# Attention steps of a two-layer kernel: the first diagonal score block moves to a place between the two transposes of the step two places before it

## The chip, the cores and the metric

The kernel runs on one core of one Trainium2 chip. The metric is the device time of one execution in microseconds (us), as the median of several runs. The engines are called PE (TensorE: matmuls and transposes), DVE (VectorE), ACT (ScalarE), POOL (GpSimd) and SP (which issues DMAs).

## What is computed

Four sequences of 512 tokens, 128 features wide, pass through four stages: relative-position attention, a mixture of 8 experts, a gated recurrence, and a mixture of 14 experts. Each adds its input and normalizes. The change touches the attention alone:

```python
q = xh @ Wq + bq;  k = xh @ Wk + bk;  v = xh @ Wv + bv          # 8 heads of 16
content = einsum('bqhd,bkhd->bhqk', q + u_bias, k)
pos_score = rel_shift(einsum('bqhd,khd->bhqk', q + v_bias, p))
attn = softmax((content + pos_score) / sqrt(e), axis=-1)
ctx = einsum('bhqk,bkhd->bqhd', attn, v) @ Wo + bo
```

The relative shift makes scores left of the diagonal, on it and right of it come from different operands, so the 512 scores of a row of queries are made in pieces.

## The kernel before

The attention is cut into 64 **steps** (STEPS). Step s takes one sequence, one group of four heads, a tile of 128 queries (number i, 0 to 3) and two of the group's heads (0 and 1 here). A head's operands lie in 32 partitions, so its score matmuls use 32 rows of the PE array, and the two heads of a step use different rows.

All engines walk one common list of events, written by `plan_attention`, and each picks out what is its own. PE's events are:

- `score s`: for each head a diagonal block of 128 columns (L892, into bank DA: head 0 in its first 128 columns, head 1 in the next), the part before the diagonal (L898, 128 x i columns) and the part from the diagonal on (L903, 512 - 128 x i columns). It is written in this order: diagonal of head 0, L898 of head 1 and of head 0, L903 of head 1 and of head 0, diagonal of head 1. The last one waits until the first has finished (s_d0), since both write the bank DA.
- `turn s, jj`: four transposes (L921) of head jj's 128x512 probabilities into bank PT. ACT copies PT to SBUF (L708). PT is a single bank, so the transposes of the next head wait for that copy (s_pTs).
- `values`: attn times v, for probabilities transposed four or more steps earlier (L936), on 32-column tiles of the array.
- `job`: projections and transposes for the next sequences and groups, on the full array (L973 to L1020).

DVE, for each score event: it copies the lower triangles of both diagonal blocks from DA over the scores (L1309, counted by s_diag), adds a correction (L1317), and takes the negated row maxima (L1321). ACT: exp of each head (L701, after DVE's maxima), the copies of PT (L708), and a few jobs. Every engine works its list in order.

In the loop of the plan, iteration s is: turn (s, 0); values; turn (s, 1); exp of step s + 1; the jobs due; score s + 2. The score event waits for exp of step s (its banks), and for s_diag, DVE's copy of step s + 1, since DA is single. For the first steps of a sequence and group it waits for the queries (s_q, s_q0) and keys (s_kb).

A fp32 matmul stands in the trace as two MATMUL rows (two passes), a transpose as one. In the first four iterations there are no values, and a matmul of no use (`warm`, L855) follows each turn.

Of the kernel before, what the change touches and what calls it, by code (L numbers as in the profile page):

```python
# [14 lines left out]
P = 128  # L15
# [5 lines left out]
NG = H // HG  # L21
# [7 lines left out]
HP = 32  # L29
STEPS = B * NG * 2 * TB  # L30
# [46 lines left out]
def plan_attention():  # L77

    jobs, plan = [], []

    def put(event):
        if event[0] == "job":
            jobs.append(event[1:])
            plan.append(("job", len(jobs) - 1))
        else:
            plan.append(event)

    per = NG * 2 * TB  # L90
    later = {}

    def at(step, *events):
        later.setdefault(step, []).extend(events)

    for e in (("stats", 0), ("cols", 0), ("kd", 0), ("job", "pem", 0), ("job", "wqT", 0), ("normz", 0), ("job", "bias", 0),
              ("job", "zT", 0), ("job", "fold", 0), ("job", "k", 0, 0), ("kb", 0, 0), ("job", "t1a", 0, 0),
              ("job", "t2a", 0, 0), ("qa", 0), ("job", "corr", 0), ("delta", 0, 0), ("job", "t1r", 0, 0),
              ("job", "t2r", 0, 0), ("kd", 1)):
        put(e)  # L100
    for i in range(1, TB):
        put(("delta", 0, i))
    at(0, ("job", "v", 0))
    at(1, ("job", "k", 0, 1), ("kb", 0, 1))
    at(2, ("job", "t1", 0, 1))
    at(3, ("job", "t2", 0, 1), ("q", 0, 1), ("xbo", 0))
    at(16, ("job", "wo", 0))
    at(6, ("numbers", 0))
    for b in range(1, B):
        base = per * (b - 1)  # L110
        first = 3 if b == 1 else 0
        at(base if b == 1 else base - 1, ("stats", b))
        at(base + first, ("normz", b))
        at(base + first + 1, ("job", "zT", b))
        at(base + first + 2, ("job", "k", b, 0), ("kb", b, 0))
        at(base + first + 3, ("job", "k", b, 1), ("kb", b, 1))
        at(base + 7, ("job", "t1", b, 0))
        at(base + 8, ("job", "t2", b, 0), ("q", b, 0))
        at(base + 9, ("job", "corr", b))
        at(base + 10, ("job", "t1", b, 1))  # L120
        at(base + 11, ("job", "t2", b, 1), ("q", b, 1))
        at(base + 13, ("job", "v", b), ("xbo", b))
    for m in range(1, B * NG):
        for i in range(TB):
            at(8 * m + 2 * i - 6, ("delta", m, i))
    for b in range(B):
        base = per * b
        at(base + 12, ("job", "ctxT", 2 * b))
        at(base + 20, ("job", "ctxT", 2 * b + 1))
        at(base + 21, ("job", "cxT", b))  # L130
        at(base + 22, ("job", "out", b), ("post", b))
        at(base + 23, ("post2", b))
        at(base + 24, ("rms", b))
        at(base + 28, ("xn2", b))
        at(base + 30, ("job", "xT", b))
        at(base + 31, ("job", "logits", b))
        at(base + 32, ("job", "rank", b))
        at(base + 33, ("scatter", b))
    plan += [("score", 0), ("exp", 0, 0), ("exp", 0, 1), ("qr", 0), ("ids", 0), ("score", 1)]
    for s in range(STEPS + 2 * per + 2):  # L140
        if s < STEPS:
            plan.append(("turn", s, 0))
        if TB <= s < STEPS + TB:
            plan.append(("values", s // TB - 1, s % TB))
            if (s // TB - 1) % 2 == 1 and s % TB == TB - 1:
                plan.append(("ctx", (s // TB - 1) // 2))
        if s < STEPS:
            plan.append(("turn", s, 1))
        if s + 1 < STEPS:
            plan += [("exp", s + 1, 0), ("exp", s + 1, 1)]  # L150
        for e in later.pop(s, []):
            put(e)
        if s + 2 < STEPS:
            plan.append(("score", s + 2))
    assert not later, later
    return jobs, plan
# [19 lines left out]
def build(nc, x_in, ca_in, ct_in, cb_in, wp0_in, wp1_in, out):  # L176
    jobs, plan = plan_attention()
# [22 lines left out]
    with ExitStack() as ctx:  # L200
# [29 lines left out]
        def by_batch(width):  # L230
            nonlocal at
            v = arena1[:, at:at + 2 * NG * width].rearrange("p (r g q) -> p r g q", r=2, g=NG)
            at += 2 * NG * width
            return v

        ka, kb, qb, qa = by_batch(S), by_batch(S), by_batch(S), by_batch(QW)
# [123 lines left out]
        s_score = sem("s_score")  # L360
        s_d0 = sem("s_d0")
        s_diag = sem("s_diag")
# [9 lines left out]
        s_q0 = sem("s_q0")  # L372
        s_q = sem("s_q")
        s_qs = sem("s_qs")
        s_kb = sem("s_kb")
# [60 lines left out]
        DA, PT, CTX, JOB = bank[4], bank[5], bank[6], bank[7]  # L436
        NHALF = STEPS // TB

        def place_of_step(s):

            m, u = divmod(s, 2 * TB)
            return m // NG, m % NG, s // TB, u // 2, 2 * (u % 2)
# [402 lines left out]
        def _(eng):  # L845
# [11 lines left out]
            def ranks(l, b, into):  # L857
# [9 lines left out]
                    mm = eng.matmul(into[:, TB * E:(TB + 1) * E], C("ones"), upto_tile[:, 0:E, TB], start=True, stop=True)  # L867
                return mm

            used = {}  # L870
            for kind, *w in plan:
                if kind == "score":
                    s = w[0]
                    b, g, _, i, j0 = place_of_step(s)
                    r = b % 2
                    if s >= 2:
                        eng.wait_ge(s_exp, 2 * (s - 2) + 2)
                    else:
                        for name in (("t1a", "t2a"), ("k", "t1r"))[s]:
                            eng.wait_ge(*after(name, 0, 0))  # L880
                    if s:
                        eng.wait_ge(s_diag, s)
                    if i == 0 and j0 == 0:
                        eng.wait_ge(*(s_q, NG * (b - 1) + g + 1) if b else (s_q0, 1 + 2 * g))
                        eng.wait_ge(s_kb, NG * b + g + 1)
                    if s == 2:
                        eng.wait_ge(s_q0, 2)
                    mine, split = slice(i * P, (i + 1) * P), i * P

                    def diagonal(jj):  # L890
                        rows = slice(HP * (j0 + jj), HP * (j0 + jj + 1))
                        return eng.matmul(DA[:, jj * P:(jj + 1) * P], qa[rows, r, g, mine], ka[rows, r, g, mine],  # L892
                                          start=True, stop=True)

                    def before(jj):
                        rows = slice(HP * (j0 + jj), HP * (j0 + jj + 1))
# [6 lines left out]
                        eng.matmul(bank[2 * (s % 2) + jj][:, split:S], qb[rows, r, g, mine], kb[rows, r, g, split:S],  # L903
                                   start=True, stop=True)

                    diagonal(0).then_inc(s_d0, 1)
                    before(1)
                    before(0)
                    behind(1)
                    behind(0)  # L910
                    eng.wait_ge(s_d0, s + 1)
                    diagonal(1).then_inc(s_score, 1)
                    if s == 0:
                        warm(1, PT[:, 0:2 * P])
                elif kind == "turn":
                    s, jj = w
# [8 lines left out]
                elif kind == "values":  # L925
                    v, t = w
                    m, hh = divmod(v, 2)
                    b, g = divmod(m, NG)
# [5 lines left out]
                    for j in range(HG):  # L934
# [3 lines left out]
                                        start=(t == 0), stop=(t == TB - 1))  # L938
                    mm.then_inc(s_pv, 1)
                elif kind == "job":  # L940
# [37 lines left out]
                    elif name == "v":  # L978
                        eng.wait_ge(*after("zT", a[0]))
                        for t in range(TB):  # L980
                            mm = eng.matmul(bk[:, t * D:(t + 1) * D], xnT[:, t * P:(t + 1) * P],
                                            A("wv").rearrange("p (h d) -> p h d", h=H)[:, :, 0:DH],
                                            start=True, stop=True)
                    elif name[0] == "t":
                        b, g = a
# [20 lines left out]
                    elif name == "out":  # L1006
                        eng.wait_ge(*after("cxT", a[0]))
                        eng.wait_ge(*after("wo", 0))
                        for t in range(TB):
                            mm = eng.matmul(bk[:, t * D:(t + 1) * D], cxT[:, t * P:(t + 1) * P], wo[:, :],  # L1010
                                            start=True, stop=True)
# [4 lines left out]
                    elif name == "logits":  # L1016
                        eng.wait_ge(*after("xT", a[0]))
                        eng.wait_ge(s_cb, 16)
                        for t in range(TB):
                            mm = eng.matmul(bk[:, t * E0:(t + 1) * E0], xnT2[:, t * P:(t + 1) * P], C("gate"),  # L1020
                                            start=True, stop=True)
# [49 lines left out]
            for kind, b, *half_of in middle:  # L1071
                r = b % 2
# [20 lines left out]
                elif kind == "gate":  # L1093
                    c = half_of[0]
                    eng.wait_ge(s_u, NC * (b + 1))
                    for q, name in enumerate(("wb", "wa", "wc")):
# [3 lines left out]
                        for k in range(NC):  # L1100
                            mm = eng.matmul(bank[4 + v % 2], R(name, k * INNER + c * P, P), uu[:, r, k, :],  # L1101
                                            start=(k == 0), stop=(k == NC - 1))
# [19 lines left out]
                elif kind == "logits":  # L1122
                    eng.wait_ge(s_copied, copied[("router", b)])
                    for t in range(TB):
                        mm = eng.matmul(bank[6][:, t * E1:(t + 1) * E1], xnT2[:, t * P:(t + 1) * P], rw[:, :],
                                        start=True, stop=True)
# [596 lines left out]
```

## Time and profile before

| | us |
|---|---|
| median of 3 runs | 553.13 (547.18 to 553.98) |
| the profiled execution, its device time | 551.84 |
| the profiled execution, its span | 550.0 |
| outside the span | 1.84 |
| from the first transposes of step 0 to those of step 62 | 19.4 to 263.5 |

The span is the time from the first instruction to the last. Rows of a timeline give start and length; the length of a PE row is modelled and includes the way through the array, so rows of pipelined matmuls overlap, and PE at 82% busy is not at its peak.

### The profile page before, as it was taken

How to read it: one execution, taken by the hardware profiler on the slowest of the kernel's cores; microseconds unless marked ns; L12 is line 12 of the kernel's file. 1: busy time of each engine (PE TensorE's matmuls, PEld its weight loads, DVE VectorE, ACT ScalarE, POOL GpSimd, SP SyncE). 2: the span in 40 equal slices, each digit the busy share in tenths (PEclk: the TensorE clock that was granted, in tenths of full speed). 3: DMA queues.
4: the chain of work that ended last, by engine and by line, in shares of the span. 5: the costliest groups of instructions: out<-in, count | busy, mean ns of one | idle time of the engine just before them, and what ended most of it. 6: DMA issues, size and time to landing. Idle time of an engine off the chain costs nothing. (4 is left out here: it accounts for less than half of the span.)

```text
span 550.0 us, 9872 instructions
## 1 busy us (share of the span) xinstructions
PE 452.6 (82%) x3109; PEld 317.3 (58%) x3109; DVE 356.1 (65%) x893; ACT 267.4 (49%) x547; POOL 249.2 (45%) x260
## 2 busy tenths in 40 slices
PE   8798999999999999999857799738979798428870
PEld 7565666656656566666434799613454466327760
DVE  4976676676876777667434466367486566638882
ACT  2356567666666565777401355517546222025653
POOL 3452563446572862440033154442445466425771
PEclk9999999999999999999886899958989978659995
DMA  8499999999999000000040230090000000013405
GB/s 308 109 174 172 170 195 345 189 190 186 194 181 159 3 1 7 16 2 1 2 143 19 63 89 28 13 378 34 0 2 1 1 21 15 24 46 77 103 19 154
DMA packets 69395, 52.72 MB, mean 96 GB/s; under 512 B 3238, under 2 KB 67245, under 8 KB 68704
## 3 DMA queue, kind: packets, MB, share of 16 engines
q1 hardware_dynamic: 66656, 47.84, 44.0%
q0 software_dynamic: 2688, 4.25, 2.6%
q8 instruction: 26, 0.43, 0.4%
q14 instruction: 25, 0.20, 0.1%
HBM read 21.30 MB, written 32.09 MB: 97 GB/s over the span
## 5 line engine op out<-in xcount | busy, mean ns | idle before, releaser
L708 ACT ACTIVATE arena<-banks 128x512 f32<-128x512 f32 x128 | 76.4, 597 | 86.3 <-PE banks L921 86.1
L921 PE MATMUL banks<-ca,work 128*128 128x128 f32 x512 | 82.2, 283 | 18.2 <-ACT arena L708 14.3
L701 ACT ACTIVATE work<-banks,nmax 128x512 f32<-128x512 f32 x128 | 80.7, 686 | 13.7 <-DVE nmax L1321 13.5
L921 PEld LDWEIGHTS banks<-ca,work 128*128 128x128 f32 x512 | 53.6, 140 | 55.5 <-issue 43.0
L1321 DVE TENSOR_REDUCE nmax<-banks 128x2 f32<-128x1024 f32 x64 | 78.3, 1224 | 2.2
L903 PE MATMUL banks<-arena 32*128 32x512 f32 (+3 forms) x256 | 60.1, 435 | 0.0
L892 PEld LDWEIGHTS banks<-arena 32*128 32x128 f32 x256 | 41.2, 184 | 30.4 <-issue 23.2
L892 PE MATMUL banks<-arena 32*128 32x128 f32 x256 | 55.2, 295 | 0.6 <-DVE corr L1401 0.6
L1309 DVE COPY_PREDICATED banks<-ca,banks 128x256 f32<-128x256 uint32 x64 | 27.2, 426 | 38.1 <-PE banks L892 37.9
L1046 PE MATMUL banks<-t,arena 128*128 128x128 f32 x300 | 47.1, 295 | 3.9 <-ACT t L815 1.0
L1101 PE MATMUL banks<-arena 128*128 128x512 f32 x96 | 45.4, 623 | 1.2 <-POOL arena L680 1.2
L1046 PEld LDWEIGHTS banks<-t,arena 128*128 128x128 f32 x300 | 40.0, 202 | 9.3 <-issue 7.6
L1055 PE MATMUL banks<-arena,work 128*128 128x128 f32 x300 | 43.3, 280 | 0.9 <-ACT work L822 0.6
L898 PE MATMUL banks<-arena 32*128 32x128 f32 (+2 forms) x192 | 43.8, 401 | 0.0
L749 ACT ACTIVATE work<-banks,arena 128x128 f32<-128x128 f32 x92 | 26.3, 368 | 31.8 <-PE banks L1046 31.8
L936 PE MATMUL banks<-arena 128*32 128x256 f32 x512 | 41.8, 402 | 0.0
L642 POOL DMA_INDIRECT returned<-arena x29 | 29.3, 1011 | 23.0 <-DVE arena L1462 13.1
L1055 PEld LDWEIGHTS banks<-arena,work 128*128 128x128 f32 x300 | 38.5, 196 | 1.7 <-ACT work L822 1.1
L547 POOL DMA_INDIRECT regions<-xc,pos x16 | 16.4, 1026 | 48.5 <-DVE pos L1202 44.7
L600 POOL TENSOR_TENSOR arena<-ca,corr 128x512 f32<-128x512 f32 x32 | 33.5, 1052 | 10.2 <-DVE nmax L1321 7.3
L633 POOL DMA_INDIRECT returned<-work,arena x23 | 22.6, 983 | 32.2 <-DVE work L1451 17.5
L903 PEld LDWEIGHTS banks<-arena 32*128 32x128 f32 x256 | 35.8, 185 | 1.0
(221 smaller groups left out, 828.9 us busy)
## 6 DMA issues: line engine op xcount, KB each, us to landing
regions<-zeros SPq DMA_DIRECT2D x15, 1040.0 KB, 18.4
regions<-zeros SPq DMA_DIRECT2D x9, 1032.0 KB, 19.9
arena<-wp_in SPq DMA_DIRECT2D x1, 4624.0 KB, 26.3
arena<-wp_in SPq DMA_DIRECT2D x1, 4494.0 KB, 15.9
arena<-ct_in SPq DMA_DIRECT2D x2, 1024.0 KB, 9.7
arena<-regions SPq DMA_DIRECT2D x29, 65.0 KB, 1.9
arena<-cb_in SPq DMA_DIRECT2D x1, 1660.0 KB, 8.2
arena<-regions SPq DMA_DIRECT2D x23, 64.5 KB, 1.9
```

What stands on the lines that cost most here:

```text
L600: eng.tensor_tensor(delta[:, i, :, :], A("ident").unsqueeze(1).broadcast_to([P, HG, P]), corr[:, b % 2, i, g * HG:(g + 1) * HG].unsqueeze( ...
L701: eng.activation(prob[:, r, :], bank[r], ACT.Exp, bias=nmax[:, s % 2, jj:jj + 1]).then_inc(s_exp, 1)
L708: eng.activation(probT[:, v % 2, j0 + jj, :, i % 2 * P:(i % 2 + 1) * P], PT.rearrange("p (t q) -> p t q", t=TB), ACT.Copy).then_inc(s_pTs, 1)
L892: return eng.matmul(DA[:, jj * P:(jj + 1) * P], qa[rows, r, g, mine], ka[rows, r, g, mine], start=True, stop=True)
L898: eng.matmul(bank[2 * (s % 2) + jj][:, 0:split], qa[rows, r, g, mine], ka[rows, r, g, 0:split], start=True, stop=True)
L903: eng.matmul(bank[2 * (s % 2) + jj][:, split:S], qb[rows, r, g, mine], kb[rows, r, g, split:S], start=True, stop=True)
L921: mm = eng.transpose(PT[:, t * P:(t + 1) * P], prob[:, 2 * (s % 2) + jj, t * P:(t + 1) * P], ident)
L936: mm = eng.matmul(CTX[HP * j:HP * (j + 1), 2 * P * hh:2 * P * (hh + 1)], vv[:, b % 2, t, h * HP:(h + 1) * HP], probT[:, v % 2, j, t, :], s ...
L1046: mm = eng.matmul(bank[r][:, c * P:(c + 1) * P], wbuf[:, r, c * P:(c + 1) * P], xTs[:, r, :], start=True, stop=True)
L1055: mm = eng.matmul(bank[3 + r][:, 0:D], hT[:, r, c * P:(c + 1) * P], wbuf[:, r, F + c * D:F + (c + 1) * D], start=(c == 0), stop=(c == CH - 1))
L1101: mm = eng.matmul(bank[4 + v % 2], R(name, k * INNER + c * P, P), uu[:, r, k, :], start=(k == 0), stop=(k == NC - 1))
L1321: eng.tensor_reduce(nmax[:, s % 2, :], pair, AX.X, ALU.max, negate=True).then_inc(count(s_fixed), 1)
```

## The change

The diagonal block of head 0 becomes an event of its own, `diag s`. It is taken out of `score s` and stands in iteration s - 2 behind turn (s - 2, 0) and the values, ahead of turn (s - 2, 1). It takes the waits for s_diag and for queries and keys with it. The rest of `score s` keeps its place, its order and the wait for exp. For steps 0 and 1 `diag` stands right ahead of `score`. No other engine's list changes.

```diff
-    plan += [("score", 0), ("exp", 0, 0), ("exp", 0, 1), ("qr", 0), ("ids", 0), ("score", 1)]
+    plan += [("diag", 0), ("score", 0), ("exp", 0, 0), ("exp", 0, 1), ("qr", 0), ("ids", 0), ("diag", 1), ("score", 1)]
     for s in range(STEPS + 2 * per + 2):
         if s < STEPS:
             plan.append(("turn", s, 0))
...
             plan.append(("values", s // TB - 1, s % TB))
...
+        if s + 2 < STEPS:
+            plan.append(("diag", s + 2))
         if s < STEPS:
             plan.append(("turn", s, 1))
...
+                if kind == "diag":
+                    s = w[0]
+                    b, g, _, i, j0 = place_of_step(s)
+                    if s:
+                        eng.wait_ge(s_diag, s)
+                    if i == 0 and j0 == 0:
+                        eng.wait_ge(*(s_q, NG * (b - 1) + g + 1) if b else (s_q0, 1 + 2 * g))
+                        eng.wait_ge(s_kb, NG * b + g + 1)
+                    if s == 2:
+                        eng.wait_ge(s_q0, 2)
+                    diagonal(s, 0).then_inc(s_d0, 1)
+                elif kind == "score":
...
-                    diagonal(0).then_inc(s_d0, 1)
                     before(1)
                     before(0)
                     behind(1)
                     behind(0)
                     eng.wait_ge(s_d0, s + 1)
-                    diagonal(1).then_inc(s_score, 1)
+                    diagonal(s, 1).then_inc(s_score, 1)
```

PE's list in the steady part, before: the transposes (L921) of a step's head 0, the values (L936), the transposes of head 1, a job (L990), the score blocks of the step two places on.

```order
L921 MATMUL banks<-ca,work 128x128 [waits s_pTs,s_exp]
L921 MATMUL banks<-ca,work 128x128 x3
L936 MATMUL banks<-arena 32x256 x4
L921 MATMUL banks<-ca,work 128x128 [waits s_pTs,s_exp]
L921 MATMUL banks<-ca,work 128x128 x3
L990 MATMUL banks<-xnT,wt 128x512 [waits s_outa,s_outd]
L892 MATMUL banks<-arena 128x128 [waits s_diag,s_exp]
L898 MATMUL banks<-arena 128x256 x2
L903 MATMUL banks<-arena 128x256 x2
L892 MATMUL banks<-arena 128x128 [waits s_d0]
```

The same place in the changed kernel, where the transposes are L927, the values L942, the job L996, the parts before and from the diagonal L905 and L910, and both diagonal blocks L875.

```order
L927 MATMUL banks<-ca,work 128x128 [waits s_pTs,s_exp]
L927 MATMUL banks<-ca,work 128x128 x3
L942 MATMUL banks<-arena 32x256 x4
L875 MATMUL banks<-arena 128x128 [waits s_diag]
L927 MATMUL banks<-ca,work 128x128 [waits s_pTs,s_exp]
L927 MATMUL banks<-ca,work 128x128 x3
L996 MATMUL banks<-xnT,wt 128x512 [waits s_outa,s_outd]
L905 MATMUL banks<-arena 128x256 [waits s_exp]
L905 MATMUL banks<-arena 128x256
L910 MATMUL banks<-arena 128x256 x2
L875 MATMUL banks<-arena 128x128 [waits s_d0]
```

The diagonal block of head 0, with its wait for s_diag, now stands ahead of the second set of transposes, and that set with everything behind it is queued behind the wait.

PE's list in iteration 0, before: both sets of transposes with their warm matmuls, the job for v (L981), the score blocks of step 2.

```order
L921 MATMUL banks<-ca,work 128x128 [waits s_exp]
L921 MATMUL banks<-ca,work 128x128 x3
L855 MATMUL banks<-ca 128x256
L921 MATMUL banks<-ca,work 128x128 [waits s_pTs,s_exp]
L921 MATMUL banks<-ca,work 128x128 x3
L855 MATMUL banks<-ca 128x256
L981 MATMUL banks<-ca,xnT 128x128 [waits s_outa,s_outd]
L981 MATMUL banks<-ca,xnT 128x128 x3
L892 MATMUL banks<-arena 128x128 [waits s_q0,s_diag,s_exp]
```

The same in the changed kernel, where the warm matmul is L857 and the job L987.

```order
L927 MATMUL banks<-ca,work 128x128 [waits s_exp]
L927 MATMUL banks<-ca,work 128x128 x3
L857 MATMUL banks<-ca 128x256
L875 MATMUL banks<-arena 128x128 [waits s_q0,s_diag]
L927 MATMUL banks<-ca,work 128x128 [waits s_pTs,s_exp]
L927 MATMUL banks<-ca,work 128x128 x3
L857 MATMUL banks<-ca 128x256
L987 MATMUL banks<-ca,xnT 128x128 [waits s_outa,s_outd]
L987 MATMUL banks<-ca,xnT 128x128 x3
L905 MATMUL banks<-arena 128x128 [waits s_exp]
```

The wait for DVE's copy of step 1 (s_diag) has moved from behind the job to ahead of the second transposes.

## Rows read from the trace of the kernel before

**Rows 1.** The page's first part: each engine's busy time and instructions.

```profile
PE 452.6 (82%) x3109; PEld 317.3 (58%) x3109; DVE 356.1 (65%) x893; ACT 267.4 (49%) x547; POOL 249.2 (45%) x260
```

**Rows 2.** Windows, the attention: length, busy by engine, then PE clock, DMA.

```profile
38.00:262.00 224.00, 210.17 (x1758) 139.92 (x1755) 160.69 (x307) 142.90 (x243) 105.42 (x106) 1.00 0.76 126
```

**Rows 3.** Waits, whole span: us in total, times, longest.

```profile
PE banks L921 <- ACT arena L708: 14.3, 64, 0.6
```

**Rows 4.** Timeline of PE, iteration 36: start, length, what [idle before].

```profile
166.33 0.66 PE L921 MATMUL banks<-ca,work 128*128 128x128 f32 x4
166.92 0.64 PE L936 MATMUL banks<-arena 128*32 128x256 f32 x8
167.77 0.63 PE L921 MATMUL banks<-ca,work 128*128 128x128 f32 x4 [0.21 <-ACT arena L708]
168.23 0.60 PE L1001 MATMUL banks<-ca,arena 128*128 128x128 f32 x4
168.76 0.37 PE L892 MATMUL banks<-arena 32*128 32x128 f32 x1
168.77 0.58 PE L898 MATMUL banks<-arena 32*128 32x384 f32 x1
168.97 0.27 PE L892 MATMUL banks<-arena 32*128 32x128 f32 x1
...
169.52 0.48 PE L903 MATMUL banks<-arena 32*128 32x128 f32 x3
...
169.85 0.27 PE L892 MATMUL banks<-arena 32*128 32x128 f32 x1
170.05 0.66 PE L921 MATMUL banks<-ca,work 128*128 128x128 f32 x4
```

**Rows 5.** Timeline of ACT, the same iteration.

```profile
167.02 0.60 ACT L708 ACTIVATE arena<-banks 128x512 f32<-128x512 f32 x1 [0.97 <-PE banks L921]
168.43 0.60 ACT L708 ACTIVATE arena<-banks 128x512 f32<-128x512 f32 x1 [0.81 <-PE banks L921]
168.93 1.26 ACT L701 ACTIVATE work<-banks,nmax 128x512 f32<-128x512 f32 x2
```

**Rows 6.** Timelines: DVE's copy in iterations 36 and 39, PE's values in 39.

```profile
166.45 0.43 DVE L1309 COPY_PREDICATED banks<-ca,banks 128x256 f32<-128x256 uint32 x1 [0.48 <-PE banks L892]
...
178.52 0.64 PE L936 MATMUL banks<-arena 128*32 128x256 f32 x8
...
178.74 0.41 DVE L1309 COPY_PREDICATED banks<-ca,banks 128x256 f32<-128x256 uint32 x1
```

**Rows 7.** Timelines of ACT and PE, an iteration without a job.

```profile
227.13 1.26 ACT L701 ACTIVATE work<-banks,nmax 128x512 f32<-128x512 f32 x2
...
227.86 0.66 PE L921 MATMUL banks<-ca,work 128*128 128x128 f32 x4
```

**Rows 8.** Timeline of PE, iterations 0 and 1.

```profile
20.86 0.63 PE L921 MATMUL banks<-ca,work 128*128 128x128 f32 x4 [0.34 <-ACT arena L708]
...
22.74 0.37 PE L892 MATMUL banks<-arena 32*128 32x128 f32 x1
...
24.83 0.65 PE L921 MATMUL banks<-ca,work 128*128 128x128 f32 x4 [0.73 <-ACT work L701]
...
26.26 0.63 PE L921 MATMUL banks<-ca,work 128*128 128x128 f32 x4 [0.34 <-ACT arena L708]
```

**Rows 9.** Timeline of DVE, its copies of steps 1, 2 and 5.

```profile
21.91 0.42 DVE L1309 COPY_PREDICATED banks<-ca,banks 128x256 f32<-128x256 uint32 x1
...
26.28 0.41 DVE L1309 COPY_PREDICATED banks<-ca,banks 128x256 f32<-128x256 uint32 x1
...
40.12 0.42 DVE L1309 COPY_PREDICATED banks<-ca,banks 128x256 f32<-128x256 uint32 x1
```

**Rows 10.** Timeline of PE, transposes in iterations 4 and 5.

```profile
39.97 0.63 PE L921 MATMUL banks<-ca,work 128*128 128x128 f32 x4 [0.21 <-ACT arena L708]
...
43.05 0.66 PE L921 MATMUL banks<-ca,work 128*128 128x128 f32 x4 [0.72 <-ACT work L701]
```

More of the change, by code:

```diff
@@ L868, in ranks, with diagonal @@
                 return mm
+            def diagonal(s, jj):
+                b, g, _, i, j0 = place_of_step(s)
+                rows, mine = slice(HP * (j0 + jj), HP * (j0 + jj + 1)), slice(i * P, (i + 1) * P)
+                return eng.matmul(DA[:, jj * P:(jj + 1) * P], qa[rows, b % 2, g, mine], ka[rows, b % 2, g, mine],
+                                  start=True, stop=True)
             used = {}
             for kind, *w in plan:
-                if kind == "score":
+                if kind == "diag":
+                    s = w[0]
+                    b, g, _, i, j0 = place_of_step(s)
+                    if s:
[7 more added lines that the diff above has]
+                elif kind == "score":
                     s = w[0]
@@ L880, in _ @@
                             eng.wait_ge(*after(name, 0, 0))
[L881 to L887, printed above, removed]
                     mine, split = slice(i * P, (i + 1) * P), i * P
[L890 to L893, printed above, removed]
                     def before(jj):
```

## The prediction

> **What bounds the kernel now.** I read the busy times first: PE is the busiest engine [rows 1], and in the attention, nearly half of the span, it has work in 210 of 224 us at a granted clock of 1.00 [rows 2], the upper level of 2.4 GHz. So the question is what PE's own sequence costs there. The list of waits gives one place in each step where PE stands still for another engine: the second transposes wait for ACT's copy of PT, 64 times, 14.3 us in all [rows 3]. The timeline of one iteration shows all of it. [rows 4] is iteration 36: transposes of head 0 at 166.33, values at 166.92, 0.21 us of idling, transposes of head 1 at 167.77, a job at 168.23, the score blocks from 168.76 to 169.85, and the next iteration's transposes at 170.05 with no wait ahead of them. ACT is not late: its copies end at 167.62 and 169.03, and the first of its two exps (1.26 us for both) ends some 0.4 us before PE needs it [rows 5]. PE's order sets the pace; only the hole ahead of the second transposes is free. The change puts a matmul into this hole.
>
> **What changing the array's shape costs, read from the same rows.** Full-array work, 32-column tiles (values) and 32-row tiles (scores) never overlap. The next kind starts 0.07 us before the modelled end of the last: transposes end at 166.99 and values start at 166.92; the job ends at 168.83 and scores start at 168.76; the diagonal ends at 170.12 and transposes start at 170.05 [rows 4]. From the last 128-column pass to the next kind is 0.20 us, where passes of 128 columns in one kind follow at 0.11.
>
> The Trainium skill has this as a rule: "TensorEngine Tiling (Array Packing)", Key Properties, says that changing the tiling mode drains the engine. The trace agrees, and puts some 0.09 us on each such drain.
>
> **The moved block, where it lands.** Values of iteration 36 end at 167.56, so by that rule of the rows the diagonal can start at 167.49. Its passes stand 0.21 us apart when it opens a kind (168.76 and 168.97 [rows 4]: its weights are not yet loaded), and 0.20 us later the transposes can start: 167.90. Before they started at 167.77. They also lose a little that the idling hid: a set that starts right behind other work takes 0.66 us and one that waited for ACT 0.63 [rows 4]. So the last transposes of head 1 come 0.13 + 0.03 = **0.16 us** later. The hole was 0.28 us wide (167.49 to 167.77) and is asked to take 0.41 and a second drain.
>
> The one unseen piece is the drain from 32-column to 32-row tiles. Bounds from the nearest rows: none at all (-0.09 us), or two drains in one (+0.09). All transitions that are shown cost the same, so I take 0.09 for this one too. Per iteration this leaves 0.07 to 0.25, about 0.16.
>
> **The block, where it is taken away: nothing comes back.** The two heads of a score event run side by side. The head-0 diagonal starts at 168.76 and L898 of head 1 at 168.77, before the diagonal's second pass at 168.97 [rows 4]. Each head has 128 + 512 = 640 columns, two passes each. At 0.107 us for 128 columns that is 1.07 us, with 0.11 for the first weights 1.18; the last pass starts at 169.85 and takes 0.11, so from 168.77 to 169.96 is 1.19. Both heads fill the whole event. After the change head 0 has 512 columns left and head 1 still 640, its diagonal among them, so the event lasts as long as before. The semaphore s_d0 was long up before head 1's diagonal, so no wait goes away either.
>
> **What stands behind the late transposes.** ACT's copy of PT, then exp of the next step on ACT, and on PE the job and the score event. With a job, PE's own sequence carries the 0.16 into the next iteration. Without one (11 iterations), the next transposes start 0.05 us after exp has ended (227.13 plus half of 1.26, about 227.8, against 227.86 [rows 7]), and exp follows the copy of PT on ACT: this path carries the 0.16 as well. Iterations 4 to 61 have both values and a moved block, 58. Iterations 4 and 5 belong to the start, which leaves 56 x 0.16 = **9.0 us**.
>
> **The moved wait.** The block waits for DVE's copy of the step before it. In iteration 36 this ends at 166.88, 0.6 us early [rows 6]. In 39 DVE has first done statistics, and the copy ends at 179.15, while the block could start at 179.16 - 0.07 = 179.09 [rows 6]; with some 0.05 us for the semaphore that is 0.12 late. The same pattern is found in 23 and 55. In 55 PE idles for exp right behind, and that hole swallows it and the iteration's 0.16. So 2 x 0.12 - 0.16 = **+0.1 us**. The queries and keys of a new group are ready many us before.
>
> At the start it costs more. DVE copies step 1 only at 21.91 to 22.33 [rows 9]; the block goes at 22.44, the second transposes of iteration 0 at 22.85 in place of 20.86, the score event at 24.76 in place of 22.74, the next transposes at 26.06 in place of 24.83 [rows 8]. Now the job for v reaches DVE 0.8 us later, so its copy of step 2, 26.28 to 26.69 [rows 9], ends at 27.49; the block follows at 27.54, and the second transposes of iteration 1 at 27.95, not 26.26 [rows 8]: 1.7 us late. In iterations 2 and 3 the block fits beside the wait for ACT. In 4 the copy ends at 40.54 [rows 9], and transposes planned for 39.97 would go at 41.0, but the next ones idle 0.72 us at 43.05 [rows 10], which takes back most; 5 has another hole. Left over: 1.7 + 0.1 = **1.8 us**, with bounds of 0.5 and 2.6, as these waits partly cover each other.
>
> **Sum.** 9.0 + 0.1 + 1.8 = 10.9 us on the profiled execution: 551.84 becomes 562.7. That execution lies 1.3 us under the median, so the forecast is 553.13 + 10.9 = **564.0 us**, 1.020 times the time before. Behind the attention nothing is due at a fixed time, so the delay is carried to the end. The bounds of the drain give 5.9 to 15.9 in place of 10.9.
>
> **Rivals.**
>
> *The hole takes the block and the score event shrinks (faster).* If the two heads' matmuls really ran one behind the other, the event would lose the first diagonal's 0.21 us and PE would get it back in the 45 iterations that PE paces. From 0.16 on, what the event gives back outweighs the late transposes. With the drain at its lower bound as well, these 45 would gain 0.21 - 0.07 = 0.14 each, 6 us, and with the start absorbed the time would be about 547; with no delay at all of the second transposes it is 45 x 0.21 = 9 us, 544. Against it: L898 of head 1 starts 0.01 us after the diagonal [rows 4]. Chance 0.07, of which 0.02 is beyond 2% (under 542.1).
>
> *A draw.* Half of that, with the event back by a part: it shrinks by about the 0.11 us of first weights, and the drain is short. The steady part costs 56 x 0.05 = 3, the start 1 to 2: 557 to 558. Chance 0.08.
>
> *Matmuls start in the order written.* Then the new order (both L898, both L903, one diagonal) overlaps badly: head 0's L903 could not start before head 1's second pass of it, and by the widths of [rows 4] the event would last 0.21 us longer (1.39 in place of 1.18, for every i). With 0.16 before it this is 0.37 in 56 iterations, 21 us, and the time about 576. Against it: L898 of head 1 at 168.77 starts ahead of the earlier written second pass at 168.97 [rows 4]. Chance 0.05.
> The Trainium skill states this rule in "TensorE: Matmul & The Clock Gate", Part 3, The mechanism: matmuls start and end strictly in program order. Here the trace disagrees, by 0.2 us in the row just named.
>
> *The waits on DVE bite more often*, since every engine's timing shifts: each stall costs 0.1 to 0.5 us; 10 of them give 566 to 569. Chance 0.10.
>
> *The change does not do what it says.* PE's list shows the block in the new place; excluded.
>
> **How the numbers follow.** The forecast has 0.70. A measurement of this kernel tells about 2%, and the forecast lies on this line: 564.2 is 2% above 553.13. Its own spread, some 3 us each way from the start-up term, the drain and the runs, falls half on each side. Within 2%: half of the forecast, the draw, the gain but for its 0.02, and 0.02 of the DVE rival: 0.50. Slower by over 2%: the other half, the order rival, the rest of the DVE rival: 0.48. Faster: 0.02. The range of 557 to 569.5 leaves out the gain, the order rival and the ends of the drain's bounds, less than 2 in 10.
>
> **What would show it.** In the changed profile the second transposes start 0.34 us after the modelled end of the values (before: 0.21), with the block between them; the score event lasts as long as before; iteration 36 lasts 3.88 us where 3.72 stands now (166.33 to 170.05 [rows 4]); the transposes of step 62 start near 274.4, not 263.5. I would be wrong if the score event got shorter by 0.1 us or more, if the transposes did not move, or if iterations 0 and 1 kept their times.

## The result

| | before | changed |
|---|---|---|
| median | 551.11 us (547.18 to 553.98, 6 runs) | 560.94 us (559.62 to 564.8, 6 runs) |
| ratio | | 1.0187, 95% interval 1.0135 to 1.0238 |
| profiled execution, span | 550.0 us | 558.4 us |
| its device time | 551.84 us | 560.2 us |

The changed kernel is slower by 9.8 us in the medians; the interval of the ratio lies on both sides of 1.02. Forecast were 10.9 us more, and 564.0 us. Of the 3.1 us between 564.0 and 560.94, 2.0 are the base: the median of three runs was 553.13, that of six is 551.11.

In two later comparisons, on other chips, the same kernel had ratios of 1.0219 (1.0145 to 1.0293) and 1.0256 (1.0202 to 1.031). The ratios leave out executions more than 1.5% above the fastest of their kernel, and in the first of the two that is four of six. The medians of all executions there are 578.69 against 560.54 us (570.09 to 595.17), and 564.74 against 549.5 us: 18.2 and 15.2 us more.

The page of the changed kernel, its first part, against [rows 1]:

```profile
PE 472.9 (85%) x3109; PEld 325.9 (58%) x3109; DVE 355.9 (64%) x893; ACT 267.0 (48%) x547; POOL 249.1 (45%) x260
```

Its windows, for the stretch from iteration 4 on that answers to [rows 2], with the same columns:

```profile
42.00:274.00 232.00, 230.81 (x1752) 147.33 (x1750) 160.38 (x306) 142.68 (x243) 105.35 (x106) 1.00 0.72 119
```

DVE, ACT and POOL are busy for as long as before. PE counts as busy in 231 of 232 us, where it was in 210 of 224 [rows 2]: its holes are gone, and the stretch is still 8 us longer. A busy share says nothing of speed when what fills a hole is dearer than what it takes away elsewhere.

The timeline of PE, iteration 36 of the changed kernel (start, length, what), answers to [rows 4]:

```profile
174.63 0.66 PE L927 MATMUL banks<-ca,work 128*128 128x128 f32 x4
175.22 0.64 PE L942 MATMUL banks<-arena 128*32 128x256 f32 x8
175.79 0.48 PE L875 MATMUL banks<-arena 32*128 32x128 f32 x2
176.20 0.66 PE L927 MATMUL banks<-ca,work 128*128 128x128 f32 x4
176.69 0.60 PE L1007 MATMUL banks<-ca,arena 128*128 128x128 f32 x4
177.22 0.91 PE L905 MATMUL banks<-arena 32*128 32x384 f32 x4
177.97 0.39 PE L910 MATMUL banks<-arena 32*128 32x128 f32 x4
178.19 0.38 PE L875 MATMUL banks<-arena 32*128 32x128 f32 x2
178.51 0.33 PE L927 MATMUL banks<-ca,work 128*128 128x128 f32 x1
```

Values end at 175.86. The block (L875) starts 0.07 us before that, and the second transposes start at 176.20, 0.34 behind the values, where it was 0.21 [rows 4]. The score event runs from 177.22 to the next transposes at 178.51, 1.29 us; with the block in it, it ran from 168.76 to 170.05, also 1.29. The iteration lasts 3.88 us (174.63 to 178.51) in place of 3.72.

The timeline of ACT in the same iteration, against [rows 5]:

```profile
175.33 0.60 ACT L710 ACTIVATE arena<-banks 128x512 f32<-128x512 f32 x1 [0.97 <-PE banks L927]
176.90 0.60 ACT L710 ACTIVATE arena<-banks 128x512 f32<-128x512 f32 x1 [0.97 <-PE banks L927]
177.39 1.26 ACT L703 ACTIVATE work<-banks,nmax 128x512 f32<-128x512 f32 x2
```

The copy of PT ends at 175.93, 0.27 us before PE is ready for the bank. PE no longer waits for ACT, and ACT idles 0.97 us for PE where it was 0.81. The list of waits, whole span as [rows 3]:

```profile
PE banks L927 <- ACT arena L710: 0.4, 2, 0.2
PEld banks L875 <- DVE banks L1315: 7.8, 10, 2.2
PE banks L875 <- DVE banks L1315: 2.8, 3, 1.4
```

The 14.3 us of waits for ACT [rows 3] have turned into 0.4. The two other rows are new: the block's weight loads wait 7.8 us in all for DVE's copy, and PE itself (PE, not PEld) stands still for it in iterations 0, 1 and 4 alone, 2.8 us.

**Where the 8.4 us between the two spans arose.** Starts of the first transposes of an iteration, from the timelines:

| | before | changed | difference, and what it grew by |
|---|---|---|---|
| iteration 0 | 19.43 | 19.08 | -0.35 |
| iteration 6 | 47.58 | 51.17 | 3.59, start-up: +3.9 |
| iteration 62 | 263.55 | 275.95 | 12.40, steady part: +8.8 |
| end of the span | 550.0 | 558.4 | 8.4, later stages: -4.0 |

The steady part was forecast at 9.1, the start-up at 1.8, the later stages at nothing.

The start of the changed kernel, timeline of PE against [rows 8] (transposes at 19.08 and 22.89 for 19.43 and 20.86):

```profile
19.08 0.79 PE L927 MATMUL banks<-ca,work 128*128 128x128 f32 x4 [1.03 <-ACT work L703]
...
22.16 0.79 PE L875 MATMUL banks<-arena 32*128 32x128 f32 x2 [1.45 <-DVE banks L1315]
22.89 1.11 PE L927 MATMUL banks<-ca,work 128*128 128x128 f32 x4
...
27.70 0.66 PE L927 MATMUL banks<-ca,work 128*128 128x128 f32 x4
```

Its windows there (length, busy of PE, PEld, DVE, ACT, POOL, then clock and DMA):

```profile
18.00:19.00 1.00, 0.05 (x2) 0.00 (x0) 0.97 (x2) 0.66 (x2) 1.00 (x2) 1.00 0.00 0
19.00:20.00 1.00, 0.92 (x5) 0.92 (x6) 0.96 (x2) 0.70 (x3) 1.00 (x2) 0.73 0.00 0
20.00:22.00 2.00, 0.72 (x2) 0.00 (x0) 1.93 (x5) 0.50 (x1) 0.52 (x1) 0.50 0.00 0
22.00:26.00 4.00, 3.84 (x15) 3.43 (x16) 1.77 (x3) 1.75 (x3) 0.00 (x0) 0.50 0.91 203
26.00:27.00 1.00, 1.00 (x9) 0.79 (x10) 0.41 (x2) 0.00 (x0) 0.00 (x0) 0.85 1.28 179
```

The block stands before the second transposes and waits for DVE, as forecast: it starts 3.08 us after the first transposes, where 3.01 was forecast (22.44 against 19.43). Not forecast: the clock is granted at 0.50, the lower level of 1.2 GHz, for 7 us from about 19.5 on. A set of four transposes takes 1.11 us in place of 0.66, and iteration 0 lasts 8.6 us (19.08 to 27.70) in place of 5.4.

### The profile page after: what moved, and what is told of

It is laid out like the page before. It is cut to its first block and busy times, and to the rows that moved or that the text cites. A ratio compares the mean times of both kernels' runs of the same rounds, so it can differ in the third digit from the quotient of the medians.

```text
span 558.4 us, 9811 instructions
## 1 busy us (share of the span) xinstructions
PE 472.9 (85%) x3109; PEld 325.9 (58%) x3109; DVE 355.9 (64%) x893; ACT 267.0 (48%) x547; POOL 249.1 (45%) x260
## 5 line engine op out<-in xcount | busy, mean ns | idle before, releaser
L927 PE MATMUL banks<-ca,work 128*128 128x128 f32 x512 | 84.5, 288 | 2.4 <-ACT work L703 1.9
L875 PEld LDWEIGHTS banks<-arena 32*128 32x128 f32 x256 | 41.5, 185 | 42.3 <-issue 28.9
L927 PEld LDWEIGHTS banks<-ca,work 128*128 128x128 f32 x512 | 53.9, 141 | 19.5 <-ACT work L703 4.4
L875 PE MATMUL banks<-arena 32*128 32x128 f32 x256 | 55.6, 296 | 3.1 <-DVE banks L1315 2.8
L910 PE MATMUL banks<-arena 32*128 32x512 f32 (+3 forms) x256 | 47.0, 440 | 0.0
L1107 PE MATMUL banks<-arena 128*128 128x512 f32 x96 | 43.0, 597 | 1.2 <-POOL arena L682 1.2
L942 PE MATMUL banks<-arena 128*32 128x256 f32 x512 | 40.5, 391 | 0.0
L1444 DVE COPY arena<-arena 128x642 f32 (+1 forms) x52 | 31.3, 601 | 6.3 <-DVE work L1457 4.0
L905 PE MATMUL banks<-arena 32*128 32x128 f32 (+2 forms) x192 | 33.7, 427 | 0.0
```

Of the source, the lines that this page charges most:

```text
L875: return eng.matmul(DA[:, jj * P:(jj + 1) * P], qa[rows, b % 2, g, mine], ka[rows, b % 2, g, mine], start=True, stop=True)
L905: eng.matmul(bank[2 * (s % 2) + jj][:, 0:split], qa[rows, r, g, mine], ka[rows, r, g, 0:split], start=True, stop=True)
L927: mm = eng.transpose(PT[:, t * P:(t + 1) * P], prob[:, 2 * (s % 2) + jj, t * P:(t + 1) * P], ident)
L942: mm = eng.matmul(CTX[HP * j:HP * (j + 1), 2 * P * hh:2 * P * (hh + 1)], vv[:, b % 2, t, h * HP:(h + 1) * HP], probT[:, v % 2, j, t, :], s ...
```

## Experiments

Twelve kernels ran, four on each of three chips. A ratio compares a kernel with the kernel before on the same chip. Iteration times are differences of timeline starts between a kernel's profile and that of the kernel before. The profiles of e1_steady and e7_not0 hold a stretch of some 14 us at half clock in the midst of the attention; "without the stretch" counts 0.16 us for each of its two iterations. On the first two of these chips iteration 50 takes 0.3 to 0.8 us more in all eight kernels than in the profile of the kernel before, which is left out as well.

**1. Same columns, other shape: e3_full and e3b_rows.** Nothing is moved; a matmul of no use stands behind the values. It waits for an exp that has long ended, not for DVE. This is e3_full; e3b_rows has `eng.matmul` of 32 rows of the same operands in place of `warm`.

```diff
                     mm.then_inc(s_pv, 1)
+                    now = TB * (v + 1) + t
+                    if now < STEPS - 2:
+                        eng.wait_ge(s_exp, 2 * now + 2)
+                        warm(1, bank[2 * (now % 2)][:, 0:P])
```

> The kernel before, with one 128-column fp32 matmul of no use on the full array put between the values and the second transposes of iterations 4 to 61; nothing is moved. Theory (what costs is the change of the array's shape and the weights that it leaves bare): the matmul has as many columns as the moved block but the shape of the transposes behind it, so it starts 0.31 us after the last pass of the values, its passes take 0.06 + 0.22, and the transposes could start at about 0.58 us, where they start now (0.59, waiting for ACT). Cost 0 to 0.01 us per iteration: the time of before. Rival (what costs is the work of the block itself): the second transposes come 0.13 us or more later as in the changed kernel, 9 us in all.

> The same addition, with the matmul on 32 rows of the array as a score block has; head 0's diagonal stays in the score event as well. Theory: a second change of shape and 0.11 us of bare weights make the second transposes start 0.72 us after the last pass of the values, and since the score event gains nothing from losing the block, adding it costs as much as moving it: 0.16 us in 58 iterations, 9 us (0.163, against 0.156 in the changed kernel). Rival (the score event does give something back): adding costs more than moving by what comes back, 0.1 us or more per iteration, so 15 us or more. It waits for no copy of DVE, so nothing of the start-up.

Iteration 36 of e3_full, timeline of PE, then of e3b_rows:

```profile
167.56 0.64 PE L936 MATMUL banks<-arena 128*32 128x256 f32 x8
168.13 0.49 PE L855 MATMUL banks<-ca 128*128 128x128 f32 x2
168.45 0.60 PE L921 MATMUL banks<-ca,work 128*128 128x128 f32 x4
```

```profile
171.50 0.64 PE L936 MATMUL banks<-arena 128*32 128x256 f32 x8
172.06 0.48 PE L944 MATMUL banks<-ca 32*128 32x128 f32 x2
172.48 0.66 PE L921 MATMUL banks<-ca,work 128*128 128x128 f32 x4
```

On the full array the filler goes in at 168.13 and the transposes follow 0.32 us later: iterations last 0.02 us more, ratio 1.0005 (0.9974 to 1.0035). On 32 rows the same columns take 0.42 us to the next start, and iterations last 0.16 us more, ratio 1.0159 (1.0082 to 1.0236). So the work of the block fits into the hole; its shape does not. My count for e3_full was 0.01 to 0.02 short. And adding costs 0.16 per iteration, as moving does, so the score event gives nothing back.

**2. The score event without the block: e4_without.** This is the kernel before without head 0's block from step 1 on; that part of the scores is left out, and the kernel serves for the time alone.

```diff
-                    diagonal(0).then_inc(s_d0, 1)
+                    if s == 0:
+                        diagonal(0).then_inc(s_d0, 1)
...
-                    eng.wait_ge(s_d0, s + 1)
+                    if s == 0:
+                        eng.wait_ge(s_d0, 1)
```

> The kernel before without the diagonal block of head 0 from step 1 on (that part of the scores is left out and replaced by what stands in the bank). Theory: head 1's 640 columns set the length of the score event, so iterations get at most 0.01 us shorter (the block's place at the event's start): the time of before within 1 us. Rival 1 (the heads run one behind the other): 0.21 us less in 45 iterations, 9 us less. Rival 2 (matmuls start in written order): the new order makes the event 0.21 us longer, 9 to 12 us more.

Iteration 36, timeline of PE:

```profile
168.87 0.92 PE L898 MATMUL banks<-arena 32*128 32x384 f32 x4
169.62 0.39 PE L903 MATMUL banks<-arena 32*128 32x128 f32 x4
169.84 0.38 PE L892 MATMUL banks<-arena 32*128 32x128 f32 x2
170.16 0.66 PE L923 MATMUL banks<-ca,work 128*128 128x128 f32 x4
```

From 168.87 to 170.16 it is 1.29 us again. Iterations are 0.00 to 0.01 us shorter, ratio 1.0006 (0.9976 to 1.0036). Taking 2 x 128 columns of PE work out of every step is worth nothing while the other head's 640 columns run beside them. Both rivals fall: neither 0.21 less nor 0.21 more.

**3. The parts of the change: e1_steady, e2_start, e7_not0.** The block is moved in iterations from 6 on (e1_steady, shown), in 0 to 3, and in all but iteration 0.

```diff
-        if s + 2 < STEPS:
+        if s + 2 < STEPS and s >= 6:
             plan.append(("diag", s + 2))
...
         if s + 2 < STEPS:
+            if s < 6:
+                plan.append(("diag", s + 2))
             plan.append(("score", s + 2))
```

> The change in iterations 6 to 61 alone; in iterations 0 to 5 the block stays in the score event. Theory: 0.156 us in 56 iterations is 8.7, with 0.25 for two late copies of DVE and 0.15 swallowed in iteration 55: 8.8 us more than before; the transposes of step 62 start 8.8 us later counted from those of step 6. The granted clock stays 1.00 in the first 280 us, since nothing waits for DVE in iteration 0. Rival (the start is what costs in the medians): under 6 us.

> The change in iterations 0 to 3 alone; from iteration 4 on the block stays in the score event. Theory (the moved wait for DVE's copy stalls PE in iterations 0 and 1, and the block is free in 2 and 3): 1.7 us later at the transposes of step 2, carried on unchanged, so 1.7 us more than before in all, 3.5 if the clock falls as well. Rival (these stalls are taken back later): under 0.5 us.

> The changed kernel, with iteration 0's block (of step 2) back in its score event. Theory: without the wait for the copy of step 1, the job for v reaches DVE on time; iteration 0 takes what it took before, and only the block of step 3 waits: the copy of step 2 ends at 26.69, so the second transposes of iteration 1 start at 27.16 in place of 26.26, and iteration 1 takes 0.9 us more. The start costs 0.9 us in place of 1.7, and 8.8 us follow. Rival (what costs in iteration 0 is the block, not the wait): iteration 1 takes what it takes in the changed kernel, and the start as much.

e1_steady: ratio 1.0124 (1.0045 to 1.0204), 563.53 to 574.77 us; from iteration 6 to 62 it takes 8.8 us more than before, without the stretch. Iterations 0 to 5 take what they took. e7_not0 has the same 8.8. The steady part adds by itself, as predicted. The expectation that the clock stays at 1.00 is refuted: in e1_steady it is 0.50 for 14 us from 198.9 on. In its profile and in that of e7_not0 it is also 0.50 for 7 us from about 8 on, before iteration 0, which starts at 22.1 and 22.8 there in place of 19.4. No moved block stands so early, so low stretches also come where the change does nothing.

e2_start: ratio 1.0112 (1.0076 to 1.0148), 5 us in the medians where 1.7 or 3.5 was expected. In its profile iteration 0 takes 3.7 us more and iteration 1 0.2, with the clock at 0.50 again; iterations 4 to 62 are as before. 4 us are so accounted for, and nothing of them is taken back.

e7_not0, iteration 1, timelines of PE and DVE:

```profile
28.32 0.66 PE L929 MATMUL banks<-ca,work 128*128 128x128 f32 x4 [0.85 <-ACT work L705]
...
30.22 0.48 PE L877 MATMUL banks<-arena 32*128 32x128 f32 x2 [0.82 <-DVE banks L1317]
30.64 0.55 PE L929 MATMUL banks<-ca,work 128*128 128x128 f32 x3
...
29.76 0.41 DVE L1317 COPY_PREDICATED banks<-ca,banks 128x256 f32<-128x256 uint32 x1
```

Between the two sets of transposes lie 2.32 us in place of 1.43 (24.83 to 26.26 [rows 8]): 0.9 more, and the block starts 0.05 us after the copy ends at 30.17. Iteration 0 takes 0.1 more. So the stalls of the start are the waits for DVE, and where the clock holds they have the forecast size. Its times, 573.86 to 580.34 with a ratio of 1.0266 (1.0214 to 1.0319), contain the half-clock stretch:

```profile
60.00:70.00 10.00, 10.00 (x80) 6.35 (x80) 6.09 (x11) 5.07 (x9) 5.17 (x4) 0.98 1.30 175
70.00:75.00 5.00, 5.00 (x20) 2.37 (x22) 1.83 (x3) 2.35 (x4) 2.49 (x3) 0.50 1.41 158
```

PE was busy throughout; iterations 10 and 11 took 3.5 and 3.1 us more.

**4. The wait alone, and the clock: e10_wait, e6_again, e11_third.** e10_wait is the kernel before with

```diff
                     s, jj = w
+                    if (s, jj) == (0, 1):
+                        eng.wait_ge(s_diag, 2)
                     eng.wait_ge(s_exp, 2 * s + jj + 1)
```

The two others are the changed kernel again.

> The changed kernel once more, beside the others of this call. Asked of it: is the low granted clock at 14 to 20 us of the changed kernel's first profile bound to the change, or chance? It fell 7 us after the 14th, before PE stood still for DVE, so by the first theory (chance) it is 1.00 here, iteration 0 takes 1.2 us more than before and iteration 1 0.4 to 0.5 more, and the transposes of step 6 start 1.7 us later than before. Rival (the wait brings it): the clock falls again, and iterations 0 and 1 take 3.2 and 0.6 us more. From the transposes of step 6 to those of step 62 it is 8.8 us more than before in either case. Ratio 1.018 to 1.022.

> The kernel before, with only the wait for DVE's copy of step 1 put ahead of the second transposes of iteration 0; no block is moved. If the wait alone is what costs in iteration 0, these transposes start at 22.44 in place of 20.86, and the transposes of step 1 come 0.8 us later at a full clock. If the stall of PE is also what takes the granted clock down in all three profiles of kernels with iteration 0's block moved, the clock is 0.50 for some 7 us between 19 and 28 us here too, and it is 3 us or more. Rival (the low clock belongs to the block or is chance): the clock stays 1.00 and the cost is 0.8 us.

> The changed kernel a third time. By what the other profiles showed: low clock near 20 us at the start, iteration 0 3 us longer or more, 8.8 us from the transposes of step 6 to those of step 62, plus 6.6 us in executions with a half-clock stretch in the attention. Theory of chance at the start: iteration 0 takes 1.2 us more.

e10_wait, timeline of PE and windows:

```profile
19.66 0.66 PE L923 MATMUL banks<-ca,work 128*128 128x128 f32 x4 [1.01 <-ACT work L701]
...
22.58 1.08 PE L923 MATMUL banks<-ca,work 128*128 128x128 f32 x4 [1.83 <-DVE banks L1311]
```

```profile
20.00:22.00 2.00, 0.75 (x5) 0.35 (x3) 1.93 (x4) 0.78 (x2) 0.94 (x1) 1.00 0.00 0
22.00:23.00 1.00, 0.42 (x2) 0.42 (x3) 0.93 (x4) 0.00 (x0) 0.00 (x0) 0.83 0.00 0
23.00:26.00 3.00, 3.00 (x14) 2.75 (x12) 1.22 (x1) 1.85 (x3) 0.00 (x0) 0.50 0.98 251
26.00:27.00 1.00, 1.00 (x11) 0.84 (x11) 0.69 (x3) 0.00 (x0) 0.00 (x0) 0.96 1.22 216
```

PE stands 1.83 us for DVE, and just behind that wait the clock goes to 0.50, with no block moved: 0.83 in the window from 22 to 23 puts the fall at about 22.7, where the transposes started at 22.58. Iteration 0 takes 2.4 us more in the profile; the medians differ by 1.8 us, ratio 1.0025 (0.998 to 1.0071), which the noise covers. All five profiles of kernels in which iteration 0 waits for DVE ahead of its second transposes (the changed kernel three times, e2_start, e10_wait) have the clock going to 0.50 between 19 and 24 us, for 3 us or more; in the other eight experiments and the kernel before it does not fall there. The expectation of chance is refuted, with one reservation: the fall does not stand in one place to the wait. It came within the wait in e2_start and e6_again (20.9 and 22.1), behind its end in e10_wait and e11_third (22.7 and 23.5), and in the first profile of the changed kernel at 19.5, before this wait and after the 1.03 us one for ACT that all kernels have. So the wait is not the only thing that counts, and how it brings the low clock is not shown.

e6_again: iterations 0 and 1 take 4.4 and 2.9 us more; ratio 1.0219. Two of its executions took 594.24 and 595.17 us at a mean granted clock of 0.877, 16 us above the profiled one (578.66, clock 0.907). They have no profile, and what they hold is open. e11_third: 2.9 and 0.05, and a second low stretch of 10 us opens at 44.0, just behind a wait of 0.84 us of iteration 4's block for DVE, and adds 2.2 and 2.6 us to iterations 4 and 5; ratio 1.0256. The same wait of 0.84 us stands in the first profile of the changed kernel and in e7_not0, and the clock stays at 1.00 there. The steady part is 8.8 in both.

**5. The added matmul again: e8_rows_again.**

> The added 32-row matmul of e3b_rows again (nothing moved). Two kernels with the moved block showed a half clock for some 14 us in the midst of the attention with PE busy throughout, which cost 6.6 us. Theory A (it comes with 32-row work between the values and the transposes, in some executions): it is found here in some executions too, and the times spread over 10 us and more. Theory B (it needs the block moved away from the score event): times within 4 us of each other, 1.016 of before.

556.5 to 559.65, ratio 1.0134 (1.0087 to 1.0182), 8.7 us from iteration 6 to 62, no half-clock stretch. This favours theory B, but with four executions on a chip where e11_third had no stretch in the steady part either, it settles nothing. Nor do the times of e3b_rows: one of its four, 572.54 at a mean clock of 0.914, lies 6.5 us above its fastest, as much as a stretch costs, but so does 564.33 (clock 0.907) among those of the kernel before on that chip. What brings the stretch stays open.

**6. Filling the hole with work of the right shape: e5_jobs and e9_jobs_all.** In the kernel before, PE alone does its job of the iteration ahead of the second transposes (e9: in iterations 0 to 3 too). The other engines' lists are untouched.

```diff
-            for kind, *w in plan:
+            early_jobs, k = list(plan), 0
+            while k < len(early_jobs):
+                if early_jobs[k][0] == "turn" and early_jobs[k][2] == 1 and TB <= early_jobs[k][1] < STEPS - 2:
+                    n = k + 1
+                    while n < len(early_jobs) and early_jobs[n][0] not in ("score", "turn"):
+                        n += 1
+                    moved = [e for e in early_jobs[k + 1:n] if e[0] == "job"]
+                    rest = [e for e in early_jobs[k + 1:n] if e[0] != "job"]
+                    early_jobs[k:n] = moved + [early_jobs[k]] + rest
+                    k = n
+                else:
+                    k += 1
+            for kind, *w in early_jobs:
```

> The kernel before with another filling for the hole: in iterations 4 to 61 PE does the iteration's job between the values and the second transposes, the score event unchanged. A job has the shape of the transposes behind it. Theory (the change of shape is what made the diagonal dear): no shape change is added, PE's sequence gets shorter by 0.28 (hole) less 0.03, but ACT's copy and exp then bind: 1.89 us from the second transposes to the next iteration, so 0.18 us less in each of 45 iterations with a job, none in the other 11: 8 us faster than before, ratio 0.985. Rival (any work in the hole delays the second transposes and with them ACT, by as much as it takes away behind them): the time of before.

> As e5_jobs, with the jobs ahead of the second transposes in iterations 0 to 3 too, where the hole is 0.34 us wide behind the warm matmul. Theory: 0.3 us less in each of iterations 1 to 3 and in iteration 0 nothing, since step 1's exp is waited for there: 1 us less than e5_jobs, ratio 0.985 to 0.988. Rival: DVE binds in these iterations, the same as e5_jobs.

Iteration 36 of e5_jobs, timeline of PE:

```profile
162.96 0.66 PE L933 MATMUL banks<-ca,work 128*128 128x128 f32 x4
163.55 0.64 PE L948 MATMUL banks<-arena 128*32 128x256 f32 x8
164.12 0.66 PE L1013 MATMUL banks<-ca,arena 128*128 128x128 f32 x4
164.62 0.60 PE L933 MATMUL banks<-ca,work 128*128 128x128 f32 x4
165.15 0.37 PE L904 MATMUL banks<-arena 32*128 32x128 f32 x1
```

The job (L1013) takes the hole and the transposes follow it without one; the iteration lasts 3.52 us in place of 3.72 (the next starts at 166.48). Most iterations with a job gain 0.10 to 0.21 us, those without mostly nothing. e5_jobs: ratio 0.9886 (0.9848 to 0.9924), 5.7 us where 8 was forecast. In its profile 43 iterations gain 7.5 us in all (0.40 in two of them, many with a long job only 0.15), 17, 32 and 34 lose 0.4, and iteration 50 of this chip takes 0.7 more. e9_jobs_all: 540.69 us against 549.5, ratio **0.9828** (0.9789 to 0.9867), with 0.2, 0.5 and 0.5 us gained in iterations 1 to 3, more than expected. It is faster than the kernel before by 1.7%, and is the change to make here.

## Why the prediction was right, step by step

- **The price of a shape change, and the landing of the block.** Forecast: block 0.07 us before the modelled end of the values, transposes 0.34 after it, 0.16 us per iteration. Measured: 0.07, 0.34, and 0.158 as the mean of the 52 iterations from 6 to 61 without 23, 32, 39 and 55. The unseen switch from 32-column to 32-row tiles costs what the seen ones do; both bounds of it fall. e3_full shows that it is the shape and not the columns.
- **Nothing comes back.** The event stays at 1.29 us with the block moved or left out (e4_without), and adding equals moving (e3b_rows). The faster rival and the draw fall. So does the one by which matmuls start in the order written: the new order did not lengthen the event.
- **What stands behind.** Iterations without a job grew by 0.16 too: ACT's copy and exp carried it.
- **The late copies.** Iterations 23 and 39 grew by 0.28, that is 0.12 beyond the 0.16, and 55 by 0.01 in place of 0.16, as forecast. 32, where DVE is late too but PE idled behind it, grew by 0.04, which I had not worked out. Sum of the steady part: 9.1 forecast, 8.8 measured.
- **The start-up, mis-sized.** Forecast 1.8 us with bounds of 0.5 and 2.6; measured 3.9, 7.5 and 7.8 in the three profiles of the changed kernel, all beyond the bounds. The waits were the right ones: iteration 0's block starts 3.08 us after the first transposes for 3.01, and with a full clock iteration 1 of e7_not0 takes the 0.9 us expected of it. What failed in this term is that it prices PE's work behind the waits at the full clock: the granted clock fell to 0.50. No run shows iteration 0 with the wait and a full clock. My rival on DVE's waits priced them at 0.1 to 0.5 us each and also without the clock.
- **The later stages.** "Carried to the end" was right for the mechanism, and wrong by 4.0 us for the two profiled executions. Windows of before, then of the changed kernel, from the transposes of step 62 on:

```profile
263.55:550.00 286.45, 207.98 (x1156) 152.37 (x1154) 168.92 (x520) 109.41 (x280) 124.34 (x125) 0.85 0.19 59
```

```profile
275.95:558.40 282.45, 202.51 (x1155) 150.18 (x1154) 168.30 (x520) 109.35 (x280) 124.33 (x125) 0.86 0.20 60
```

The same instructions, 5.5 us less of PE busy, at a mean clock of 0.86 for 0.85 (the column before the last two). The clock changes between its levels many times in these stages, and their length varies with it: in e8, e10, e11 and e9, whose code is the same there, on one chip, it is 282.0, 283.6, 284.5 and 286.1 us. I read the 4.0 us as this variation. It fits that the changed kernel is not the shortest on the other chips either: 284.5 (e11) among those four, and 295.5 (e6) where the three others of that chip have 294.2 to 297.2. Argued, not shown: no run shifted these stages alone.

So the total of 10.9 against 9.8 measured is closer than its parts: 2.1 us too little at the start and 4.0 us of luck with the clock behind it, in the executions that were profiled. Of the chances, "within 2%" held in the first comparison, by a ratio whose interval crosses 1.02, while the later ones lie at 1.022 and 1.026, with the costs of a low clock on top. There the medians grew by 18.2 and 15.2 us, and 10.9 would have been too little.

## What to carry to other kernels

A hole on an engine is only as wide as the work around it allows: on PE count the drain and the bare weights of each change of the array's shape, and fill the hole with work that has the shape of a neighbour. Before moving work off a stretch, see which of the parallel chains in it is the longest; taking from the other one gives nothing. A wait moved forward on a PE that runs at the full clock can cost twice, once in itself and once in a low clock around it.

## What was unexpected in the hardware

- A stall of 1.4 to 2.0 us on PE at the start of the attention came with 3 to 14 us at a granted clock of 0.50, in 5 of 5 profiles; the 1.0 us idling before it in all kernels did not bring it in the others. In e10_wait this is worth more than the wait itself (2.4 us where 0.8 was worked out).
- In some executions of kernels with the moved block the clock was 0.50 for some 14 us in the midst of the attention, with PE busy in 5.0 of 5.0 us of the windows. It cost 6 us in each of the two profiles that show it. Its cause is open.
- Matmuls on different 32-row tiles did not start in the order written: head 1's pass at 168.77 stands ahead of head 0's earlier written second pass at 168.97 [rows 4], and in the changed kernel's new order (two blocks each of 128i and 512 - 128i columns, then one diagonal) the event kept its 1.29 us.
